# A gated-delta layer: another order within a wave, masks and reductions moved, and layer norms with narrow reciprocals

## The chip, the cores and the metric

The kernel runs on one core of a Trainium2 chip. It is one program of some 48,000 instructions: a model of four layers, all in fp32. The metric is the device time in microseconds. An execution of the kernel before took 2885.48 us (median of three runs, 2884.47 to 2887.69).

## The reference

The input is x of 2 x 512 tokens with 256 channels. Each layer is `x = x + attention(norm(x)) + ffn(norm(x))`. Three layers and all feed-forward parts stay as they are; the change touches the norm, which stands ahead of each layer, and the attention of the last layer, a gated delta rule with 16 key heads, 32 value heads and head width 128:

```python
def _layernorm(x, axis=-1, eps=1e-05):
    m = jnp.mean(x, axis=axis, keepdims=True)
    v = jnp.var(x, axis=axis, keepdims=True)
    return (x - m) / jnp.sqrt(v + eps)
...
            L = -jnp.matmul(kbc, jnp.swapaxes(kc, -1, -2), precision=prec) * decay
            L = jnp.where(tri_incl, 0.0, L)
            attn = solve_triangular(eye - L, jnp.broadcast_to(eye, L.shape), lower=True)
...
                a_i = jnp.matmul(q_i, jnp.swapaxes(k_i, -1, -2), precision=prec) * dm_i
                v_new = v_i - jnp.matmul(kcd_i, state, precision=prec)
                out_i = jnp.matmul(q_i * jnp.exp(g_i)[..., None], state, precision=prec) + jnp.matmul(a_i, v_new, precision=prec)
                new_state = state * jnp.exp(g_last)[..., None, None] + jnp.matmul(jnp.swapaxes(k_i * jnp.exp(g_last[..., None] - g_i)[..., None], -1, -2), v_new, precision=prec)
...
        xf = core.astype(jnp.float32) * jax.nn.silu(z.astype(jnp.float32))
        var = jnp.mean(xf * xf, axis=-1, keepdims=True)
        xf = xf * jax.lax.rsqrt(var + EPS) * norm_weight
        return out @ W_out
```

Queries, keys and values go through a convolution of four taps and a silu first.

## The kernel before, in words

The kernel runs its stages one after the other (`build`). Each norm (`layer_norm`) multiplies with a constant matrix, which puts the mean, and then the variance, of each token on all 128 partitions; ScalarE takes the root of 512 columns at once (L113), VectorE the reciprocal (L94) and the product (L99).

The delta layer (`delta_attention`) works in 64 waves: 16 key heads, and for each four chunks of 128 tokens (CH = 4). A wave holds PR = 4 matrices of 128 x 128: two batches by two value heads. Its steps reach over four turns of the main loop, so in the turn w each engine works for waves w+2, w, w-1 and w-2:

- wave w+2 is made: gates (L1458) and scores (L1468, L1470) on TensorE, `low` (L1871) on VectorE, `decay` and `grown` (L1689, L1692) on ScalarE, then on VectorE `at` and `rough` (L1879), products of the scores with the decay, and `v0` (L1888), the triangular matrix to be inverted, from `rough` and a strict mask. Values and keys are transposed (L1477, L1483) and copied.
- SyncE spreads `v0` through DRAM (L1348, L1354, L1362), so that GpSimd can invert the 16 x 16 diagonal blocks by substitution on 32 partitions (L1823 to L1835, 28 dependent steps and a copy), and gathers the blocks (L1371, L1377).
- for wave w VectorE widens the gathered blocks (L1901) and TensorE joins them to 32, 64 and 128 columns: join_a (L1494), close_a, join_b, close_b, join_c, close_c (L1548), each with copies by ScalarE and VectorE between. The last copy (L1722) gives the inverse.
- for wave w-1 come recall (L1557), rest (L1926), solve (L1565), new values (L1727), the answer (L1575, L1576) and the state's growth (L1582, L1946), the gated output `xf` (L1936), its squares (L1734), their sum (L1953, L1955) and the root to the power -0.5 on GpSimd (L1813).
- for wave w-2 VectorE scales `xf` (`normed`, L1959), TensorE transposes and projects it (L1591, L1602), and VectorE adds it to x (L1967).

Beside this the projections of the next head (L1418, L1428) run as up to four parts a wave, in the PSUM banks BG and BK that the gates and scores of the wave have left. A wave has three parts where w % 4 is 2 or 3, two where it is 0 and four where it is 1; from the last heads on there are none. In the same way VectorE does the four taps of one convolution a wave (L1854, L1857); where w % 4 is 2 its parts come late in the turn.

The order of each engine is written out by hand, as calls in the loop over w. Every engine takes its instructions in this order, and a wait holds all behind it. TensorE's order before is:

```python
make(w + 2); recall(w - 1); join_a(w); part(w, 0)
solve(w - 1); turn_values(w + 2); close_a(w); part(w, 1)
answer(w - 1); join_b(w); part(w, 2); turn_keys(w + 2)
close_b(w); turn_out(w - 2); part(w, 3)
join_c(w); project_out(w - 2); close_c(w)
```

## Time and profile before

| | |
|---|---|
| median of three runs | 2885.48 us (2884.47 to 2887.69) |
| the profiled execution's own time | 2888.33 us |
| its span | 2886.6 us |
| mean granted TensorE clock over the span | 0.907 |
| TensorE busy | 2389.7 us, 83% |
| VectorE busy | 1545.3 us, 54% |
| ScalarE busy | 931.0 us, 32% |
| GpSimd busy | 985.5 us, 34% |

The profiled execution is 2.85 us above the median. Its 1.7 us outside the span stand for what lies around the program. Busy time is an average over all stages, and a busy TensorE can be one at half clock, so the table alone says little of the delta layer; the stretch from 1299.7 to 2811 us is that layer's main loop.

### The profile page before, as it was taken

Reading aid. Unit: us, or ns where it says so; the run is one execution under the profiler, and the core shown is the slowest. Engines: PE = TensorE matmul, PEld = TensorE weight load, DVE = VectorE, ACT = ScalarE, POOL = GpSimd, SP = SyncE. Lnnn points to the kernel's source line nnn. Section 1 sums busy time; section 2 is a strip of 40 time slices with the busy share of each in tenths; the row PEclk is TensorE's granted clock in tenths of the full one; section 3 lists DMA queues with packets and bytes.
Section 4 is the critical chain, followed back from the end, with each engine's and each line's share of the span. In section 5 each row is a group of like instructions: output and inputs, shape, how many; then the busy total and the mean of one; then the engine's idle time right before and its main releaser. Section 6 shows DMA issues by size and latency. Waiting matters only on the chain. (4 is left out here: it accounts for less than half of the span.)

```text
span 2886.6 us, 48059 instructions
## 1 busy us (share of the span) xinstructions
PE 2389.7 (83%) x18052; PEld 1459.9 (51%) x18052; DVE 1545.3 (54%) x2863; ACT 931.0 (32%) x1896; POOL 985.5 (34%) x2123
## 2 busy tenths in 40 slices
PE   6597999986897958747888888888888888888879
PEld 3234444433332425334566656666666666666753
DVE  1632555657753142335666666666666666666531
ACT  1162111101152122123444434444444434443421
POOL 1310001110002001305555555555555555555520
PEclk8798999998798989967999999999999999999989
DMA  1002010101001000011111111111111111111100
GB/s 48 1 0 76 22 37 28 44 0 35 1 1 45 0 28 17 16 31 34 23 36 34 35 27 27 35 37 27 28 35 36 27 34 27 35 38 21 26 13 15
DMA packets 183490, 78.06 MB, mean 27 GB/s; under 512 B 133200, under 2 KB 164464, under 8 KB 183152
## 3 DMA queue, kind: packets, MB, share of 16 engines
q1 hardware_dynamic: 183280, 75.23, 10.0%
q8 instruction: 136, 2.23, 0.3%
q14 instruction: 74, 0.61, 0.1%
HBM read 52.10 MB, written 22.02 MB: 26 GB/s over the span
## 5 line engine op out<-in xcount | busy, mean ns | idle before, releaser
L1832 POOL TENSOR_TENSOR a_z<-a_z,a_term 32x14 f32<-32x14 f32 (+6 forms) x896 | 342.8, 383 | 70.2
L1828 POOL TENSOR_TENSOR a_term<-a_z,a_l 32x14 f32<-32x14 f32 (+6 forms) x896 | 333.6, 372 | 70.2
L1418 PE MATMUL ps<-all_xn,a_w_qkv 128*128 128x512 f32 x512 | 311.4, 743 | 6.2 <-ACT a_grown L1692 4.1
L1005 POOL TENSOR_TENSOR all_x<-all_x,f_part_out 128x512 f32<-128x512 f32 x64 | 85.0, 1365 | 634.3 <-DVE f_part_out L977 634.3
L878 PE MATMUL ps<-all_xn,f_w 128*128 128x512 f32 x640 | 287.8, 594 | 1.9 <-ACT f_share L896 1.9
L1857 DVE SCALAR_TENSOR_TENSOR a_qkv<-a_raw,a_taps,a_qkv 128x1024 f32<-128x1024 f32 x192 | 245.2, 1277 | 2.5
L1823 POOL TENSOR_TENSOR a_z<-a_l,a_ident 32x256 f32<-32x256 f32 x64 | 47.0, 735 | 563.7 <-DMA a_l<-a_v_dram 563.7
L878 PEld LDWEIGHTS ps<-all_xn,f_w 128*128 128x128 f32 x640 | 122.2, 191 | 155.8 <-issue 155.8
L1666 ACT ACTIVATE a_raw<-ps 128x512 f32<-128x512 f32 x128 | 76.5, 597 | 365.8 <-PE ps L1418 365.8
L1494 PE MATMUL ps<-a_t_wide,a_v_off 32*32 32x32 f32 x2048 | 33.9, 211 | 179.9 <-DVE a_t_wide L1901 179.9
L864 PE MATMUL ps<-f_gated,f_w 128*128 128x512 f32 x320 | 155.1, 612 | 20.9 <-DVE f_part_out L977 20.9
L985 DVE TENSOR_TENSOR f_gated<-f_act_h,ps 128x512 f32<-128x512 f32 x80 | 55.0, 688 | 215.0 <-ACT f_act_h L901 214.8
L901 ACT ACTIVATE f_act_h<-ps 128x512 f32<-128x512 f32 x80 | 47.8, 597 | 375.8 <-PE ps L878 375.8
L1428 PE MATMUL ps<-a_w_z,all_xn 128*128 128x256 f32 x512 | 153.3, 453 | 16.8 <-ACT a_zs L1670 16.8
L1602 PE MATMUL ps<-a_out_t,a_w_out 128*128 128x256 f32 x512 | 133.4, 405 | 40.3 <-ACT a_out_t L1740 26.3
L1418 PEld LDWEIGHTS ps<-all_xn,a_w_qkv 128*128 128x128 f32 x512 | 104.1, 223 | 97.2 <-issue 92.0
L1936 DVE SCALAR_TENSOR_TENSOR a_xf<-ps,a_zs 128x512 f32<-128x512 f32 x64 | 44.2, 691 | 190.2 <-PE ps L1576 190.2
L1915 DVE COPY a_za<-ps 32x128 f32<-32x128 f32 x128 | 37.1, 290 | 182.8 <-PE ps L1510 181.9
L1494 PEld LDWEIGHTS ps<-a_t_wide,a_v_off 32*32 32x32 f32 x2048 | 26.1, 122 | 205.6 <-DVE a_t_wide L1901 205.6
L1428 PEld LDWEIGHTS ps<-a_w_z,all_xn 128*128 128x128 f32 x512 | 110.3, 226 | 36.0 <-ACT a_zs L1670 17.2
L1602 PEld LDWEIGHTS ps<-a_out_t,a_w_out 128*128 128x128 f32 x512 | 95.7, 197 | 59.2 <-ACT a_out_t L1740 31.1
L864 PEld LDWEIGHTS ps<-f_gated,f_w 128*128 128x128 f32 x320 | 61.6, 195 | 102.9 <-issue 72.8
(261 smaller groups left out, 4903.3 us busy)
## 6 DMA issues: line engine op xcount, KB each, us to landing
a_v_dram<-a_v SPq DMA_DIRECT2D x64, 256.0 KB, 2.0
f_w<-in_f_w SPq DMA_DIRECT2D x24, 512.0 KB, 4.9
a_w_qkv<-in_a_w SPq DMA_DIRECT2D x16, 512.0 KB, 3.8
a_t_dram<-a_z SPq DMA_DIRECT2D x512, 8.0 KB
a_w_z<-in_a_w SPq DMA_DIRECT2D x16, 256.0 KB, 2.8
a_w_out<-in_a_wo SPq DMA_DIRECT2D x16, 256.0 KB, 2.8
a_v_off<-a_v SPq DMA_DIRECT2D x256, 4.0 KB, 1.8
a_l<-a_v_dram SPq DMA_DIRECT2D x256, 8.0 KB
```

The costliest lines, as they stand in the source:

```text
L864: mm = pe.matmul(ps[:, 4 + b * KC + m, :], w2[:, v, f, m * P:(m + 1) * P], gated[:, (v * TILES + i) % 4, :], start=f == 0, stop=f == FT - 1)
L878: mm = pe.matmul(ps[:, bank + n % 2, :], w[:, v, k, f * P:(f + 1) * P], xn[:, k, b * T:(b + 1) * T], start=k == 0, stop=k == KC - 1)
L985: dve.tensor_tensor(gated[:, n % 4, :], act_h[:, n % 2, :], ps[:, 2 + n % 2, :], ALU.mult).then_inc(gated_ready, 1)
L1005: pool.tensor_tensor(part, part, part_out[:, n, :], ALU.add).then_inc(added, 1)
L1418: mm = pe.matmul(ps[:, to, :], w_qkv[:, k, mt * P:(mt + 1) * P], xn[:, k, b * T:(b + 1) * T], start=k == 0, stop=k == KC - 1)
L1428: mm = pe.matmul(ps[:, to, i * 256:(i + 1) * 256], xn[:, k, tt * P:(tt + 1) * P], w_z[:, k, :], start=k == 0, stop=k == KC - 1)
L1494: mm = pe.matmul(narrow(BW)[q, r, :], v0_off[q, w % 3, r, :], t_wide[q, 1, r, :], start=True, stop=True)
L1602: mm = pe.matmul(bank(BO)[:, B * m:B * (m + 1), :], w_out[:, v, m * P:(m + 1) * P], out_t[:, v::VPK, :], start=v == 0, stop=v == VPK - 1)
L1666: act.activation(raw[:, mt, b, TAPS - 1:], ps[:, of, :], ACT.Copy).then_inc(raw_ready, 1)
L1828: pool.tensor_tensor(term[:, 0:j, j + 1:], z[:, 0:j, j:j + 1].broadcast_to([HP, j, n]), rows[:, j:j + 1, j + 1:].broadcast_to([HP, j, n]), ...
L1832: pool.tensor_tensor(z[:, 0:j, j + 1:], z[:, 0:j, j + 1:], term[:, 0:j, j + 1:], ALU.add).then_inc(sub_step, 1)
L1857: dve.scalar_tensor_tensor(to, rows, tap, to, ALU.mult, ALU.add).then_inc(conv_ready if j == TAPS - 1 else conv_step, 1)
```

## The change

In the loop over w the order of all engines changes. TensorE's `make` is cut in two (`make_gates`, `make_scores`), `answer` in three (`ask`, `answer`, `grow_state`). `rough` and its product go: `v0` is made from the scores in PSUM, the factor and `decay`. This leaves ones' places on its diagonal filled, and GpSimd sets the diagonal to 1.0 after copying the blocks. `at` is made after `v0`. The sums of squares come from an accumulator of ScalarE's Square, one instruction for each of the four matrices. `normed` moves from VectorE to GpSimd, behind `root`. In the norm, variance, root and reciprocal work on one column per 128 tokens, and a product with the identity spreads the result over the partitions in PSUM.

The new orders, as loop bodies (each call stands under its own condition; `late` is w % 4 == 2):

```python
# TensorE
make_gates(w + 2); recall(w - 1); make_scores(w + 2); ask(w - 1)
turn_values(w + 2); solve(w - 1); part(w, 0); join_a(w)
grow_state(w - 1); close_a(w); answer(w - 1); join_b(w)
part(w, 1); close_b(w); turn_out(w - 2); part(w, 2)
turn_keys(w + 2); join_c(w); project_out(w - 2); part(w, 3); close_c(w)
# ScalarE
make_decay(w + 2); grow(w + 2); new_values(w - 1); part(w, 0); copy_tb(w)
make_values(w + 2); silu 0; copy_wb(w); part(w, 1); copy_half(w)
copy_out(w - 2); square(w - 1); silu 1; copy_wc(w); silu 2; part(w, 2)
silu 3; copy_whole(w); part(w, 3); make_keys(w + 2)
# VectorE
make_low(w + 2); make_right(w - 1); make_v0(w + 2); widen(w); make_at(w + 2)
close_wa(w); make_qg(w + 2); copy_za(w); carry(w - 1); gated(w - 1)
conv 0 (late: conv 0, 1, 2); copy_z_half(w); conv 1, 2, 3 (late: none)
reduce(w - 1); late: conv 3; add_out(w - 2)
# GpSimd
substitute(w + 2); root(w - 1); normed(w - 1)
```

The core of the diff:

```diff
@@ layer_norm, TensorE, VectorE, ScalarE @@
-                    for k in range(KC):
-                        mm = pe.matmul(ps[:, B + b, :], mean_of[:, :], square[:, k, b * T:(b + 1) * T],
-                                       start=k == 0, stop=k == KC - 1)
+                    for tt in range(b * ST, (b + 1) * ST):
+                        for k in range(KC):
+                            mm = pe.matmul(ps[:, B + b, tt:tt + 1], square[:, k, tt * P:(tt + 1) * P],
+                                           mean_of[:, 0:1], start=k == 0, stop=k == KC - 1)
+                for b in range(B):
+                    pe.wait_ge(rstd_ready, b + 1)
+                    for q in range(ST):
+                        tt = b * ST + q
+                        mm = pe.matmul(ps[:, 2 * B + b, q * P:(q + 1) * P],
+                                       rstd[:, tt:tt + 1].to_broadcast([P, P]), ident[:, :], start=True, stop=True)
+                    mm.then_inc(spread, 1)
-                    dve.reciprocal(std[:, b, :], std[:, b, :]).then_inc(rstd_ready, 1)
+                    dve.reciprocal(rstd[:, of], rstd[:, of]).then_inc(rstd_ready, 1)
-                        dve.tensor_tensor(xn[:, k, part], xn[:, k, part], std[:, b, :],
+                        dve.tensor_tensor(xn[:, k, part], xn[:, k, part], ps[:, 2 * B + b, :],
-                    act.activation(std[:, b, :], ps[:, B + b, :], ACT.Sqrt,
+                    act.activation(rstd[:, of], ps[:, B + b, of], ACT.Sqrt,
@@ delta_attention, TensorE @@
                 def turn_values(w):
                     if w >= 1:
                         pe.wait_ge(krow_ready, PR * w)
+                    if w % CH == 0:
+                        pe.wait_ge(qkv_ready, 4 * (w // CH) + 3)
-                def answer(w):
-                    pe.wait_ge(vnew_ready, PR * (w + 1))
-                    pe.wait_ge(at_ready, w + 1)
+                def ask(w):
+                    pe.wait_ge(state_ready, PR * (w + 1))
                     pe.wait_ge(qg_ready, w + 1)
                     if w >= 2:
                         pe.wait_ge(added, w - 1)
                     for r in range(PR):
-                        pe.matmul(bank(BO)[:, r, :], qg[:, w % 4, r, :], state[:, r, :], start=True, stop=False)
+                        mm = pe.matmul(bank(BO)[:, r, :], qg[:, w % 4, r, :], state[:, r, :],
+                                       start=r == 0, stop=False)
+                    mm.then_inc(asked, 1)
+
+                def answer(w):
+                    pe.wait_ge(vnew_ready, PR * (w + 1))
+                    pe.wait_ge(at_ready, w + 1)
+                    for r in range(PR):
                         mm = pe.matmul(bank(BO)[:, r, :], at[:, w % 4, r, :], v_new[:, r, :],
-                                       start=False, stop=True)
+                                       start=False, stop=r == PR - 1)
                     mm.then_inc(o_psum, 1)
+
+                def grow_state(w):
                     if w % CH == CH - 1:
                         return
+                    pe.wait_ge(vnew_ready, PR * (w + 1))
@@ project_out @@
                     pe.wait_ge(ot_ready, w + 1)
+                    if w >= 1:
+                        pe.wait_ge(added, w)
@@ ScalarE, square @@
-                    act.activation(sq[:, :, :], xf[:, :, :], ACT.Square).then_inc(sq_ready, 1)
+                    for r in range(PR):
+                        act.activation(sq[:, r, :], xf[:, r, :], ACT.Square,
+                                       accum_out=sums[:, r:r + 1]).then_inc(sq_ready, 1)
@@ GpSimd @@
+                def normed(w):
+                    pool.wait_ge(rstd_ready, w + 1)
+                    if w >= 1:
+                        pool.wait_ge(ot_psum, w)
+                    pool.tensor_tensor(xnorm[:, :, :], xf[:, :, :],
+                                       rstd[:, :].unsqueeze(2).broadcast_to([P, PR, P]), ALU.mult
+                                       ).then_inc(xnorm_ready, 1)
-                    pool.tensor_tensor(z16[:, w % 2, 0, :], l16[:, w % 2, :], ident16[:, :],
-                                       ALU.add).then_inc(sub_step, 1)
+                    pool.tensor_copy(z16[:, w % 2, 0, :], l16[:, w % 2, :]).then_inc(sub_step, 1)
+                    pool.wait_ge(sub_step, steps * w + 1)
+                    pool.memset(z16[:, w % 2, 0, ::SB + 1], 1.0).then_inc(sub_step, 1)
@@ VectorE @@
                 def make_v0(w):
-                    dve.wait_ge(rough_ready, w + 1)
+                    dve.wait_ge(kq_ready, w + 1)
+                    dve.wait_ge(decay_ready, w + 1)
                     for r in range(PR):
-                        dve.scalar_tensor_tensor(v0[:, w % 3, r, :], rough[:, r, :], gate(K_NBETA, w, r),
-                                                 strict[:, :], ALU.mult, ALU.mult).then_inc(v0_ready, 1)
+                        dve.scalar_tensor_tensor(v0[:, w % 3, r, :], bank(BK)[:, r // VPK, :], gate(K_NBETA, w, r),
+                                                 decay[:, r, :], ALU.mult, ALU.mult).then_inc(v0_ready, 1)
@@ carry @@
                     if w % CH == CH - 1:
+                        dve.wait_ge(asked, w + 1)
                         dve.memset(state[:, :, :], 0.0).then_inc(state_ready, PR)
@@ reduce @@
-                    dve.tensor_reduce(var[:, :], sq[:, :, :], AX.X, ALU.add).then_inc(var_step, 1)
-                    dve.wait_ge(var_step, w + 1)
-                    dve.tensor_scalar(var[:, :], var[:, :], 1.0 / P, 1e-6, ALU.mult, ALU.add).then_inc(var_ready, 1)
+                    dve.tensor_scalar(var[:, :], sums[:, :], 1.0 / P, 1e-6, ALU.mult, ALU.add).then_inc(var_ready, 1)
@@ build @@
+                sp.dma_start(ident[:, :], d["ident"]).then_inc(arrived, 16)
```

## Rows read from the trace of the kernel before

**Rows 1.** Windows: busy us and instructions of each engine, clock, DMA share, GB/s.
```profile
1351.10:2683.50 1332.40, 1137.28 (x13005) 862.56 (x13003) 851.71 (x1838) 576.79 (x1286) 755.28 (x1787) 0.92 0.14 31
```
**Rows 2.** Timeline of TensorE: start us, us, the gates' product, first of a wave.
```profile
1351.12 1.24 PE L1458 MATMUL ps<-a_upto,a_gates 128*128 128x128 f32 x8
...
2683.48 1.16 PE L1458 MATMUL ps<-a_upto,a_gates 128*128 128x128 f32 x8
```
**Rows 3.** Waits, 1320 to 2720 us: total us, times, longest.
```profile
PE ps L1494 <- DVE a_t_wide L1901: 171.2, 60, 8.9
```
**Rows 4.** Timeline of TensorE over one wave with four projections.
```profile
2013.80 0.45 PE L1494 MATMUL ps<-a_t_wide,a_v_off 32*32 32x32 f32 x32 [2.75 <-DVE a_t_wide L1901]
2014.18 3.68 PE L1428 MATMUL ps<-a_w_z,all_xn 128*128 128x256 f32 x8
...
2024.75 1.99 PE L1428 MATMUL ps<-a_w_z,all_xn 128*128 128x256 f32 x8
2026.58 0.38 PE L1483 MATMUL ps<-a_ident,a_qkv 128*128 128x128 f32 x2
...
2032.71 1.16 PE L1458 MATMUL ps<-a_upto,a_gates 128*128 128x128 f32 x8
2033.71 0.61 PE L1468 MATMUL ps<-a_qkv 128*128 128x128 f32 x4
...
2038.38 0.65 PE L1494 MATMUL ps<-a_t_wide,a_v_off 32*32 32x32 f32 x32 [2.74 <-DVE a_t_wide L1901]
```
**Rows 5.** Timelines of ScalarE (first line) and VectorE (the others), one wave.
```profile
2049.38 0.62 ACT L1734 ACTIVATE a_sq<-a_xf 128x512 f32<-128x512 f32 x1
...
2057.59 1.12 DVE L1871 SCALAR_TENSOR_TENSOR a_low<-ps,a_gates,a_floor 128x128 f32<-128x128 f32 x4
2059.25 1.12 DVE L1926 SCALAR_TENSOR_TENSOR a_rest<-ps,a_gates,a_v_row 128x128 f32<-128x128 f32 x4 [0.53 <-PE ps L1557]
...
2060.89 0.68 DVE L1879 TENSOR_TENSOR a_rough<-ps,a_decay 128x512 f32<-128x512 f32 x1
2061.48 0.41 DVE L1901 TENSOR_TENSOR a_t_wide<-a_t_narrow,a_side 128x256 f32<-128x256 f32 x1
```
**Rows 6.** Timelines of SyncE, GpSimd and VectorE; last line: durations min/median/max of L1005.
```profile
2039.40 0.34 SPq L1348 DMA_DIRECT2D a_v_dram<-a_v  x1
...
2044.98 5.99 SPq L1371 DMA_DIRECT2D a_t_dram<-a_z  x8
2046.32 0.72 POOL L1823 TENSOR_TENSOR a_z<-a_l,a_ident 32x256 f32<-32x256 f32 x1 [8.43 <-DMA a_l<-a_v_dram]
...
2049.61 0.27 POOL L1828 TENSOR_TENSOR a_term<-a_z,a_l 32x50 f32<-32x50 f32 x1
...
2052.35 0.36 SPq L1377 DMA_DIRECT2D a_t_narrow<-a_t_dram  x1
...
2056.40 1.28 DVE L1857 SCALAR_TENSOR_TENSOR a_qkv<-a_raw,a_taps,a_qkv 128x1024 f32<-128x1024 f32 x1
2056.54 1.30 POOL L1832 TENSOR_TENSOR a_z<-a_z,a_term 32x50 f32<-32x50 f32 x1
...
2061.01 1.01 POOL L1813 TENSOR_TENSOR a_rstd<-a_var,a_half 128x4 f32<-128x4 f32 x1
...
L1005 POOL TENSOR_TENSOR all_x<-all_x,f_part_out x64: 1261/1271/2297, 346.8 to 1208.2; 128x512 f32<-128x512 f32 x64
```
**Rows 7.** Timeline of TensorE: two waves without projections.
```profile
2701.92 1.16 PE L1458 MATMUL ps<-a_upto,a_gates 128*128 128x128 f32 x8
...
2720.23 1.16 PE L1458 MATMUL ps<-a_upto,a_gates 128*128 128x128 f32 x8
```
**Rows 8.** Timeline of the last norm.
```profile
1218.86 1.28 ACT L113 ACT_TABLE_LOAD   x1
...
1218.90 1.98 PE L79 MATMUL ps<-n_square,all_mean_of 128*128 128x512 f32 x4 [0.25 <-ACT n_square L108]
...
1220.88 3.35 DVE L94 RECIPROCAL n_std<-n_std 128x512 f32<-128x512 f32 x1 [2.70 <-ACT n_std L113]
...
1228.86 1.29 DVE L99 TENSOR_TENSOR all_xn<-all_xn,n_std 128x512 f32<-128x512 f32 x2
```

More of the change, by code:

```diff
@@ L92, in _ @@
                 for b in range(B):
+                    of = slice(b * ST, (b + 1) * ST)
                     dve.wait_ge(std_ready, b + 1)
-                    dve.reciprocal(std[:, b, :], std[:, b, :]).then_inc(rstd_ready, 1)
-                    dve.wait_ge(rstd_ready, b + 1)
+                    dve.reciprocal(rstd[:, of], rstd[:, of]).then_inc(rstd_ready, 1)
+                for b in range(B):
+                    dve.wait_ge(spread, b + 1)
                     dve.wait_ge(squared, KC * (b + 1))
@@ L1249, in delta_attention @@
         zs = s.buf("zs", [P, 2, TT, VPK * P])
-        low, decay, grown, rough = (s.buf(n, [P, PR, P]) for n in ("low", "decay", "grown", "rough"))
+        low, decay, grown = (s.buf(n, [P, PR, P]) for n in ("low", "decay", "grown"))
         v0, v0_off = s.buf("v0", [P, 3, PR, P]), s.buf("v0_off", [P, 3, PR, HP])
@@ L1460, in make, with make_scores @@
                     mm.then_inc(gc_ready, 1)
+                def make_scores(w):
+                    before = parts_of(w - 3)
                     if before:
@@ L1463, in make @@
                     elif w >= 1:
-                        pe.wait_ge(rough_ready, w)
+                        pe.wait_ge(v0_ready, PR * w)
+                        pe.wait_ge(at_ready, w)
                     if w % CH == 0:
@@ L1626, in _ @@
                     if made(w + 2):
-                        make(w + 2)
+                        make_gates(w + 2)
                     if made(w - 1):
                         recall(w - 1)
+                    if made(w + 2):
+                        make_scores(w + 2)
+                    if made(w - 1):
+                        ask(w - 1)
+                    if made(w + 2):
+                        turn_values(w + 2)
+                    if made(w - 1):
+                        solve(w - 1)
+                    part(w, 0)
                     if made(w):
                         join_a(w)
-                    part(w, 0)
                     if made(w - 1):
-                        solve(w - 1)
-                    if made(w + 2):
-                        turn_values(w + 2)
+                        grow_state(w - 1)
                     if made(w):
                         close_a(w)
-                    part(w, 1)
                     if made(w - 1):
@@ L1643, in _ @@
                         join_b(w)
+                    part(w, 1)
+                    if made(w):
+                        close_b(w)
+                    if made(w - 2):
+                        turn_out(w - 2)
                     part(w, 2)
@@ L1647, in _ @@
                     if made(w):
-                        close_b(w)
-                    if made(w - 2):
-                        turn_out(w - 2)
-                    part(w, 3)
-                    if made(w):
                         join_c(w)
@@ L1655, in _ @@
                         project_out(w - 2)
+                    part(w, 3)
                     if made(w):
@@ L1801, in _ @@
                         copy_whole(w)
+                    part(w, 3)
+                    if made(w + 2):
+                        make_keys(w + 2)
             @block.gpsimd
@@ L1830, in substitute @@
                                            ALU.mult).then_inc(sub_step, 1)
-                        pool.wait_ge(sub_step, steps * w + 2 * j)
+                        pool.wait_ge(sub_step, steps * w + 2 * j + 1)
                         pool.tensor_tensor(z[:, 0:j, j + 1:], z[:, 0:j, j + 1:], term[:, 0:j, j + 1:],
@@ L1842, in _ @@
                         root(w - 1)
+                        normed(w - 1)
             @block.vector
@@ L2010, in _ @@
                 for w in range(-2, W + 2):
+                    late = w % CH == 2
                     if made(w + 2):
@@ L2019, in _ @@
                     if made(w + 2):
-                        make_v0(w + 2)
-                    if made(w - 2):
-                        normed(w - 2)
+                        make_at(w + 2)
                     if made(w):
                         close_wa(w)
-                    late = w % CH == 2
-                    if not late:
-                        conv(w, 0)
+                    if made(w + 2):
+                        make_qg(w + 2)
                     if made(w):
```

129 lines of the change are left out of this document (65 added, 64 removed).

## Prediction

> **What bounds the kernel now.** The windows view comes first. It shows the delta layer's steady part, from 1351.1 to 2683.5, as 1332.4 us in which TensorE is busy 1137, GpSimd 755, VectorE 852 and ScalarE 577, at a mean granted clock of 0.92 [rows 1]: TensorE is nearest to full, and it is the one whose stalls I look for. The marks that bound this part are the same instruction, the first of a wave, 57 waves apart [rows 2]: 1332.4 / 57 = 23.4 us a wave. In the waits of this stretch TensorE has one long one, at the join of the inverse (L1494) for the widened blocks (L1901): 171.2 us in 60 times, 2.85 each [rows 3].
>
> TensorE's timeline shows the rest of that stall [rows 4]. The wave from 2013.80 to 2038.38 (24.58 us, four projections) holds the idle gap of 2.74, and the projection right behind the gap takes 3.68 where the same work takes 1.99 later in the wave. Double the time is the lower of the two clock levels, 1.2 in place of 2.4 GHz: behind each gap TensorE works at half clock, and 1.69 more is lost. What is left, 24.58 - 2.74 - 1.69 = 20.15, is the wave's work at full clock. Two of the four kinds of wave have one projection less (1.83, from 2024.75 to 2026.58), so 18.3; one has two less and no state growth (as many passes as the gates' product, 1.0 from 2032.71 on), so 15.5. The mean of the four is **18.07 us**: TensorE's floor, 5.3 below today's wave.
>
> Why TensorE waits: VectorE makes low, rest, at and rough and only then widens, 2057.59 to 2061.48, 3.89 us with 0.5 of waiting for the recall in it [rows 5]. TensorE has only scores and recall to do beside that.
>
> **The change, part by part.**
>
> *The order within a wave.* I lay the steps on a line from the end of close_c, with these durations. TensorE: gates to 1.0, recall 1.9, scores 2.8, ask 3.7, values turned 4.2. VectorE: low 1.1 to 2.2, rest to 3.3, v0 to 4.4 (ScalarE's decay, of the size of the 0.62 square, lies beside rest), widen to 4.8. The solve wants rest (3.3) and finds it; then comes the first projection, 5.1 to 6.9, which wants grown (3.5); the join then wants the widened blocks (4.8). **The stall is gone, with 2 us to spare**: widening moved up on VectorE, and the join moved behind ask, values, solve and a projection. In one wave of four ScalarE reloads a table ahead of the exponential, 1.28 [rows 8], which moves v0 and widen to 5.7, still ahead of the join. Without the gap there is no half clock. Further down each copy now has a product of another chain in front of the product that wants it: projection 1 between join_b and close_b, projection 2 or the keys between turn_out and project_out. I followed all waits: new_values ends at 6.4, growth wants it at 7.3; the gated output is done near 11.5, project_out wants it at 16; VectorE's add_out ends near 0.5 of the next wave, the ask wants it at 2.8. So the new waits (ask and project_out on the add, carry on the ask, turn_values on the keys, which ScalarE now copies last) find their semaphore up. Queued behind them, if not: behind the ask the solve, and with it everything; behind carry VectorE's gated output. What is late next is rest, 0.9 ahead of the solve. In every fourth wave, the one with late convolutions, copy_z_half stands behind three of them, near 16.8, and close_c wants it at 17.7.
>
> Gain: 57 x (23.4 - 18.07) = 302 us at the floor. For hand-overs that my line has too smooth I charge 0.4 a wave, 23 us: **279**.
>
> *VectorE's load.* rough (0.68) goes; v0 reads PSUM and decay in place of rough and mask, in four instructions like low's (1.12): the same. The reduction and the normed output go as well, tiles of rough's size. 852 / 57 = 14.9 a wave less 3 x 0.68 is 12.9, under 15.5 even with gaps: this is cover, not a term. It is worth 0 while TensorE bounds; if it were missing, the short wave would wait for VectorE by 1 to 2 us.
>
> *Sums of squares on ScalarE.* One instruction of 0.62 [rows 5] becomes four with an accumulator, a form the trace lacks. Bounds: 0 more, and 4 x 0.62 - 0.62 = 1.9. I take 0.6, since each works on a quarter and only its start is paid four times. ScalarE is busy 577 of 1332, so it hides: 0.
>
> *GpSimd.* It gets the normed output; the same tile in a two-input operation costs 1.27 at the median and 2.3 at most [rows 6]; I take 1.3, these being the same size. The identity addition becomes a copy and a small memset: even. Its wave was 2046.32 to 2061.01, 14.7, and 1.0 for the root; it becomes 14.7 + 1.0 + 1.3 + small gaps = **17.1**, 95% of TensorE's 18.07. It starts 6.9 behind the first DMA of its wave (2039.40 to 2046.32). So normed ends 6.9 + 17.1 = 24 behind v0, near 10.5 of the next wave, where gated (10.7) just finds it; in short waves gated waits 1 to 2 us, which VectorE's slack takes. SyncE issues the same DMAs in the same order; none is moved past another. Price 0, with rival A below.
>
> On the port the trace shows contention: a 50-element GpSimd operation takes 1.30 beside VectorE's convolution step and 0.27 alone [rows 6]. The Trainium skill ("SBUF — State Buffer", section "SBUF: two separate sides") calls the shared port pair an exclusive lock, held for the whole instruction, so that the other side fully blocks. It speaks against moving work to GpSimd: by that rule a convolution that meets the normed output waits for it, up to 1.3 on VectorE a wave, and with VectorE at 12.9 + 1.3 the sum stays as it is.
>
> *Waves without projections.* The last ones took 18.3 (2701.92 to 2720.23) [rows 7], mostly latency. On the same line they come to 14.3, and GpSimd, without three stretched steps, to 14.7 - 3 + 1.0 + 1.3 = 14. Four of them, and a little in the four that drain: **17** (10 to 25). The first two waves wait for the first inverse as before: 0.
>
> *The four norms.* The last part is a reciprocal over 512 columns, 3.35 us, twice, and four products, 1220.88 to 1230.15 [rows 8]. Now root and reciprocal take four columns, TensorE turns the result into rows (eight passes a half, like the gates' product, 1.0), and the products read PSUM. The line: table loaded 1220.1, variances of the second half to 1220.8, spread to 1221.8 and 1222.8, products to 1224.4: 5.7 saved. At half clock the narrow products double, and 3.6 is saved. x4: **22** (14 to 23). The identity's load at the start rides beside the 1 MB of x: 0 to 1.
>
> *Sum*, against the profiled execution's own 2888.3: 2888.3 - 279 - 17 - 22 = 2570. That execution is 2.8 above the median of the runs; taken off, the forecast is **2568 us**. The rivals below are on the same footing.
>
> **The rivals.**
>
> *A. GpSimd becomes the bound.* For it: 17.1 against 18.07, and steps stretched by 1 us; the normed output could meet convolutions and take 2.3. Then GpSimd's wave is 18.1, and with what the chain gated, convolutions, low, v0 adds some 19.5: 57 x 3.9 = 222, sum 2624. Against: VectorE drops two operations that used the port.
>
> *B. A stall of some 2 us comes back elsewhere*, at the solve (for rest) or the ask (for the add), with half clock behind it: 21 a wave, 57 x 2.4 = 137, sum 2709. For it: VectorE's chain add, low, rest has under 1 us to spare. Against: the line above.
>
> *C. The order brings nothing*, because the wave is really held by the round of v0: 6.9 to GpSimd, 14.7 of steps, then the stores and the load (2044.98 to 2052.35, 7.4, and 2 to land [rows 6]), 31 us over two waves, 15.5 a wave. That is below 18, so it can hardly hold; only the norms would gain, 2863.
>
> *D. Slower.* One place: the normed output on GpSimd, behind the dependent steps and the root. It decides where GpSimd's wave passes 24.1, today's wave plus what tail and norms give back: 24.1 - 15.8, so 8.3 us for that operation. The root of only four elements costs 1.01 [rows 6], so GpSimd's prices can surprise; at 10 us the wave is 25.8, 2885.5 + 57 x 2.4 - 39 = 2983. Against it stands the 1.27 of a tile of the same size.
>
> **Chances.** Forecast 0.58; A 0.23; B 0.13; C 0.03; D 0.02; 0.01 for the rest. The forecast's own range is 2537 (no charge for hand-overs, 25 in the tail) to 2600. Taking in A with its spread gives 2537 to 2660, with B, C and D outside. Slower is D, 0.02; within 0.2% (5.8 us, about what a measurement of this kernel can tell from no change) 0.01; faster 0.97.
>
> **What the profile of the changed kernel would show.** TensorE's wait for widen gone; the gates' first marks 18 to 19 apart on average, 15.5 to 20 by kind of wave; granted clock near 1.0 in the steady part; all projections at 1.83; GpSimd busy over 85% of it, its DMA wait under 2 us a wave; VectorE's gated output waiting for the normed one in some waves; normed at 1.3; each norm near 13.5 from first product to last. The forecast is wrong if TensorE shows a new idle of 2 us a wave before solve, ask or project_out, or if GpSimd has no wait for its DMA left.

## The result, and the profile after

| | before | after |
|---|---|---|
| median | 2886.56 us (4 runs, 2884.47 to 2887.69) | 2551.61 us (4 runs, 2546.98 to 2560.84) |
| ratio, 95% interval | | 0.8844 [0.8818, 0.8871] |
| profiled execution: time, span | 2888.33, 2886.6 | 2553.82, 2552.0 |
| granted clock over the span | 0.907 | 0.939 |

335 us are gone; 318 were forecast (2885.5 to 2568), and 2551.6 lies inside the range. The kernel after was timed again later (after_again): 2552.16 us (5 runs), ratio 0.8837 [0.8825, 0.8850]. To read the numbers below one thing is needed: 13 of the 58 executions of kernels with the new norm, and none of the 57 with the old one, took 20 to 27 us more than their kernel's others, in the two that were profiled ahead of the last norm, for a cause that no run here isolates (it may be a price of the new norm), so where a kernel's spread is wide I read its delta layer from the profile.

The windows view after, with the columns of [rows 1]. The first stretch is the filling of the delta layer, the second its 57 steady waves, the third the rest of its loop, the waves without projections and the draining ones:

```profile
1285.60:1333.90 48.30, 33.01 (x242) 19.24 (x242) 23.71 (x46) 14.14 (x30) 26.62 (x73) 0.79 0.12 25
1333.90:2372.50 1038.60, 1032.51 (x13004) 805.08 (x13002) 753.88 (x1669) 616.84 (x1684) 804.58 (x1884) 1.00 0.18 41
2372.50:2476.50 104.00, 87.27 (x1286) 74.33 (x1284) 48.95 (x142) 47.02 (x157) 56.98 (x157) 0.95 0.11 23
```

The 57 waves of [rows 1] took 1332.4 us and now take 1038.6, 18.22 each in place of 23.4. TensorE is busy 1032.5 us of them at a granted clock of 1.00, the upper level; before it was busy 1137.3 at 0.92. So both parts of the old stall went: 195.1 us of idle time (1332.4 - 1137.3) are down to 6.1, and 104.8 us of busy time (1137.3 - 1032.5) are gone too, for as many instructions, so it is what the half clock had added. The 335 us split, by the two profiles, into waves 293.8, everything ahead of the loop 14.1 (it starts at 1285.61 in place of 1299.72), filling 3.1 and tail 23.6.

TensorE's timeline of a short wave, a gates' product to the next, to be held against [rows 4]:

```profile
1972.61 1.16 PE L1473 MATMUL ps<-a_upto,a_gates 128*128 128x128 f32 x8
...
1976.69 1.06 PE L1586 MATMUL ps<-a_rest,a_inv 128*128 128x128 f32 x8
1977.59 1.88 PE L1432 MATMUL ps<-all_xn,a_w_qkv 128*128 128x512 f32 x4
1979.40 0.45 PE L1515 MATMUL ps<-a_t_wide,a_v_off 32*32 32x32 f32 x32
1980.28 0.45 PE L1527 MATMUL ps<-a_t_wide,a_wa 32*32 32x32 f32 x32 [0.42 <-DVE a_wa L1964]
...
1988.65 1.16 PE L1473 MATMUL ps<-a_upto,a_gates 128*128 128x128 f32 x8
```

The join (L1515) stands 6.8 us behind the wave's start and waits for nothing. The only idle time is 0.42 at close_a (L1527), for the copy of the join's own result: this wave has no growth between the two. The four waves from 1954.29 on take 18.32, 16.04, 20.08 and 18.32; by kind I had read 18.3, 15.5, 20.15 and 18.3 out of [rows 4].

VectorE's timeline (first line: widen in the wave that starts at 1954.29; second line: the copy behind join_a), and the waits of the steady part:

```profile
1958.60 0.41 DVE L1956 TENSOR_TENSOR a_t_wide<-a_t_narrow,a_side 128x256 f32<-128x256 f32 x1
...
1961.61 0.29 DVE L1964 TENSOR_TENSOR a_wa<-ps,a_ident 128x128 f32<-128x128 f32 x1 [2.00 <-PE ps L1515]
```

```profile
DVE a_wa L1964 <- PE ps L1515: 97.6, 57, 2.4
POOL a_z L1875 <- DMA a_l<-a_v_dram: 96.9, 37, 5.5
...
DVE a_xf L1991 <- POOL a_xnorm L1863: 21.5, 21, 1.7
```

Widen ends 4.7 us behind the wave's start (4.8 on my line), 2 us ahead of the join. The direction of the wait of [rows 3] has turned: it is VectorE that now waits for the join, 1.7 us a wave, while TensorE idles 6.1 us in the 57 waves together. GpSimd still waits for its DMA, 96.9 / 57 = 1.7 us a wave, so it is no bound. VectorE waits for the normed output 21 times, 21.5 us in all.

GpSimd's timeline shows what was given to it:

```profile
1961.65 1.01 POOL L1857 TENSOR_TENSOR a_rstd<-a_var,a_half 128x4 f32<-128x4 f32 x1
1962.74 1.04 POOL L1863 TENSOR_TENSOR a_xnorm<-a_xf,a_rstd 128x512 f32<-128x512 f32 x1
1966.42 0.39 POOL L1875 COPY a_z<-a_l 32x256 f32<-32x256 f32 x1 [2.63 <-DMA a_l<-a_v_dram]
...
1982.91 0.39 POOL L1875 COPY a_z<-a_l 32x256 f32<-32x256 f32 x1
```

The wave from the first copy to the second is 16.5 us long (17.1 forecast), and GpSimd waits for nothing in it.

The last norm, against [rows 8]:

```profile
1199.37 6.39 PE L76 MATMUL ps<-all_x,all_mean_of 128*128 128x512 f32 x8 [7.17 <-PEq L41]
...
1205.60 1.84 PE L83 MATMUL ps<-all_mean_of,n_square 128*128 128x1 f32 x16
...
1207.80 3.17 PE L83 MATMUL ps<-all_mean_of,n_square 128*128 128x1 f32 x16 [0.36 <-ACT n_square L121]
...
1210.83 3.76 PE L90 MATMUL ps<-all_ident,n_rstd 128*128 128x128 f32 x16
1211.01 0.26 ACT L127 ACTIVATE n_rstd<-ps,n_eps 128x4 f32<-128x4 f32 x1 [1.68 <-PE ps L83]
1211.30 0.18 DVE L106 RECIPROCAL n_rstd<-n_rstd 128x4 f32<-128x4 f32 x1 [1.77 <-ACT n_rstd L127]
1212.92 1.28 DVE L112 TENSOR_TENSOR all_xn<-all_xn,ps 128x512 f32<-128x512 f32 x2 [1.44 <-PE ps L90]
1214.63 1.28 DVE L112 TENSOR_TENSOR all_xn<-all_xn,ps 128x512 f32<-128x512 f32 x2 [0.42 <-PE ps L90]
```

The windows view over the second half's variances and over the spread (the clock is the third number from the end):

```profile
1208.00:1211.00 3.00, 3.00 (x17) 3.00 (x17) 0.18 (x1) 1.31 (x2) 0.00 (x0) 0.54 0.02 5
1211.00:1215.00 4.00, 3.59 (x16) 3.30 (x16) 1.83 (x4) 0.26 (x1) 0.00 (x0) 0.50 0.00 0
```

The reciprocal of 3.35 us is down to 0.18. But sixteen one-column passes of the variance take 3.17 us the second time and 1.84 the first, and the spread (L90), sixteen passes of a kind of which eight take 1.0 in a wave, takes 3.76. The granted clock is 1.00 from 1205.6 to 1208, then 0.54 and 0.50: the spread stands at half clock, and so does nearly all of the second half's variance. This norm takes 16.5 us from its first product to the end of its last multiplication, 19.3 before. It is the one of the four that gained least: the others take 14.0, 13.7 and 12.4 us in place of 19.2, 19.2 and 17.4.

### The profile page after: what moved, and what is told of

Same layout as the page of the kernel before. It is cut to its first block and busy times, and to the rows that moved or that the text cites. A ratio compares the mean times of both kernels' runs of the same rounds, so it can differ in the third digit from the quotient of the medians.

```text
span 2552.0 us, 49069 instructions
## 1 busy us (share of the span) xinstructions
PE 2292.4 (90%) x18212; PEld 1420.6 (56%) x18212; DVE 1403.0 (55%) x2671; ACT 973.6 (38%) x2344; POOL 1046.1 (41%) x2251
## 5 line engine op out<-in xcount | busy, mean ns | idle before, releaser
L1432 PE MATMUL ps<-all_xn,a_w_qkv 128*128 128x512 f32 x512 | 251.0, 617 | 5.3 <-ACT a_grown L1733 4.0
L1442 PE MATMUL ps<-a_w_z,all_xn 128*128 128x256 f32 x512 | 125.9, 390 | 16.8 <-ACT a_zs L1708 16.8
L1432 PEld LDWEIGHTS ps<-all_xn,a_w_qkv 128*128 128x128 f32 x512 | 90.6, 195 | 78.5 <-issue 76.7
L1442 PEld LDWEIGHTS ps<-a_w_z,all_xn 128*128 128x128 f32 x512 | 96.0, 195 | 29.7 <-ACT a_zs L1708 17.2
L1768 ACT ACTIVATE a_v_new<-ps,a_gates 128x128 f32<-128x128 f32 x256 | 73.2, 368 | 91.7 <-PE ps L1586 91.6
L1925 DVE SCALAR_TENSOR_TENSOR a_low<-ps,a_gates,a_floor 128x128 f32<-128x128 f32 x256 | 72.0, 344 | 63.3 <-PE ps L1473 63.3
L1875 POOL COPY a_z<-a_l 32x256 f32<-32x256 f32 x64 | 26.5, 414 | 189.8 <-DMA a_l<-a_v_dram 189.6
L587 POOL TENSOR_TENSOR a_heads<-a_mixed,a_recip 128x512 f32<-128x512 f32 x8 | 10.1, 1268 | 226.6 <-DVE a_recip L653 226.6
L280 ACT ACTIVATE a_probs<-ps 128x512 f32<-128x512 f32 x128 | 65.8, 606 | 78.6 <-PE ps L245 78.6
```

What stands on the lines that cost most here:

```text
L1432: mm = pe.matmul(ps[:, to, :], w_qkv[:, k, mt * P:(mt + 1) * P], xn[:, k, b * T:(b + 1) * T], start=k == 0, stop=k == KC - 1)
L1442: mm = pe.matmul(ps[:, to, i * 256:(i + 1) * 256], xn[:, k, tt * P:(tt + 1) * P], w_z[:, k, :], start=k == 0, stop=k == KC - 1)
L1768: act.activation(v_new[:, r, :], bank(BR)[:, r, :], ACT.Copy, scale=gate(K_BETA, w, r)).then_inc(vnew_ready, 1)
L1925: dve.scalar_tensor_tensor(low[:, r, :], bank(BG)[:, r, :], gate(K_GC, w, r), floor[:, :], ALU.subtract, ALU.min).then_inc(low_ready, 1)
```

## The experiments

Each is named by its label. Line numbers shift by a few between kernels. The ratio is against the kernel before, 0.8844 being the change's own. "Steady part" is the stretch of the 57 waves, 1038.6 us in the change. Each diff shows the core of its edit.

**norms_only.** The kernel before with the new norm and nothing else.

```diff
 # before, layer_norm as in the change
+        ident = s.buf("ident", [P, P])
+                sp.dma_start(ident[:, :], d["ident"]).then_inc(arrived, 16)
-                sp.wait_ge(arrived, 32)
+                sp.wait_ge(arrived, 48)
```

> The kernel before with the new layer norm and nothing else. Theory (the profile after): each norm gives back 3.3 us and not 5.7, since the narrow products run at half clock; four of them give 13, so 2873 us against 2886.5. Rival (the term as it was summed): 22, so 2864. A third: the gain of the norms is inside the delta layer too, by the clock that it starts with: over 25.

Measured: 2872.76 us (12 runs), ratio 0.9971 [0.9946, 0.9997], 14 less than the 2886.81 measured beside it. That agrees with the first theory's 13, but not with its "3.3 us each": in this kernel's profile the norms take 16.5, 13.4, 12.3 and 16.5 us, 2.6, 5.7, 5.1 and 2.7 less than before. So the gain is not the same at each place.

**full_var.** The change, with 128 equal columns moving in the variance products where it has one. ScalarE reads one in 128 of them.

```diff
-                            mm = pe.matmul(ps[:, B + b, tt:tt + 1], square[:, k, tt * P:(tt + 1) * P],
-                                           mean_of[:, 0:1], start=k == 0, stop=k == KC - 1)
+                            q = tt - b * ST
+                            mm = pe.matmul(ps[:, B + b, q * P:(q + 1) * P], square[:, k, tt * P:(tt + 1) * P],
+                                           mean_of[:, :], start=k == 0, stop=k == KC - 1)
-                    act.activation(rstd[:, of], ps[:, B + b, of], ACT.Sqrt,
+                    act.activation(rstd[:, of], ps[:, B + b, ::P], ACT.Sqrt,
```

> The kernel after with one thing changed in the norm: the variance's products take 128 equal columns of the mean matrix as the moving side instead of one, at the same number of passes, and ScalarE reads one column of each. Theory (the narrow products leave TensorE's array so little to do that the clock falls behind them): the passes stay at 0.11 us, the clock stays up, the spread takes 1.9 and not 3.8 us, and 2 to 3 us are saved in each norm, 8 to 12 in all, 2542. Rival (the clock falls for another reason, so wide passes at half clock cost what they did): 0 to 4 us more. The difference is near what a comparison can tell, so the norm's own rows decide.

The timeline of its last norm (L84 the variances, L91 the spread):

```profile
1205.90 2.05 PE L84 MATMUL ps<-all_mean_of,n_square 128*128 128x128 f32 x16 [0.26 <-ACT n_square L122]
...
1207.79 1.95 PE L91 MATMUL ps<-all_ident,n_rstd 128*128 128x128 f32 x16
...
1208.89 2.48 DVE L113 TENSOR_TENSOR all_xn<-all_xn,ps 128x512 f32<-128x512 f32 x4 [0.42 <-PE ps L91]
```

Products 128 times as wide take less time: 2.05 in place of 3.17, and the spread behind them 1.95 in place of 3.76. The granted clock is 1.00 from 1205.90 to 1211.00, where the change had 0.54 and 0.50. So it was the narrow products, by the clock behind them, that had cost the last norm its missing time: it takes 13.8 us here and 16.5 in the change. The whole kernel: 2547.54 us (5 runs), ratio 0.8827 [0.8815, 0.8839], 4.6 under the change timed beside it; the two intervals overlap, so the rows are the proof and not the median. The forecast of 8 to 12 was too high, for it took every norm to lose what the last one does: the four take 13.6, 13.8, 11.6 and 13.8 us, 3.9 less in all, 2.7 of it in the last. It is the fastest version of this study.

**widen_early.** The kernel before with one call moved: widening ahead of the scores' copies on VectorE.

```diff
+                    if made(w):
+                        widen(w)
                     if made(w + 2):
                         make_scores(w + 2)
-                    if made(w):
-                        widen(w)
```

> The kernel before with one call moved: VectorE widens ahead of at and rough, so the join's wait should fall from 2.85 us to some 1.5. Theory (clock follows the gap's length): a gap of 1.5 us leaves TensorE at full clock, so 1.3 + 1.7 = 3.0 us a wave, 57 waves, some 170 us and about 2715 us in all. Rival (any gap in front of the join halves the clock behind it): only 1.3 a wave, 75 us, 2810. Rival of no gain: at and rough, later by 0.4, hold the next projection: under 20 us.

Measured: 2793.91 us (4 runs, 2784.19 to 2799.68), ratio 0.9684 [0.9668, 0.9701], 93 less; the profiled execution is the fastest of the four. Its timeline of TensorE, its waits and the window of its 57 steady waves:

```profile
1897.74 0.45 PE L1494 MATMUL ps<-a_t_wide,a_v_off 32*32 32x32 f32 x32 [1.55 <-DVE a_t_wide L1901]
1898.13 1.98 PE L1418 MATMUL ps<-all_xn,a_w_qkv 128*128 128x512 f32 x4
```

```profile
PE ps L1494 <- DVE a_t_wide L1901: 89.5, 57, 2.0
...
DVE a_xnorm L1959 <- POOL a_rstd L1813: 38.2, 32, 3.7
...
PE ps L1506 <- DVE a_wa L1909: 35.1, 32, 3.5
```

```profile
1351.99:2577.90 1225.91, 1063.00 (x13005) 820.81 (x13003) 863.60 (x1838) 581.27 (x1286) 752.76 (x1780) 0.98 0.15 34
```

The gap shrank from 2.75 to 1.55, and the projection behind it takes 1.98, not 3.68: behind the shorter gap TensorE kept the upper clock. By both together 3 us a wave should have gone, 170 in all. In this profile's steady part 106 went (1332.4 - 1225.9), 1.9 a wave: 74 as busy time (1137.3 - 1063.0) and 32 as idle time, for the join's wait fell by 67 (156.9 in the same stretch before), and 35 came back as a new wait, close_a for wa (L1506). It comes from VectorE, which waits 38.2 us for GpSimd's root ahead of that very wa (L1959), 4.7 before. The median lies near the rival's 2810, but the rows are against that rival, since the clock behind the join stayed up. One call moved gives about a third of the gain; the rest is in the other moves.

**join_early.** The change with the join moved up behind the ask, ahead of the values, the solve and the projection.

```diff
-                    if made(w):
-                        join_a(w)
                     if made(w - 1):
                         grow_state(w - 1)
...
                         ask(w - 1)
+                    if made(w):
+                        join_a(w)
                     if made(w + 2):
                         turn_values(w + 2)
```

> The kernel after with one call moved back: join_a behind ask, ahead of the transposed values, the solve and the first projection. The widened blocks are ready 4.7 us into a wave and the ask ends at 3.6, so TensorE idles 1.1 (2 where the table is reloaded), 1.35 on average. Theory (short gaps keep the clock): 57 x 1.35 = 77 us more than the kernel after, 2630. Rival (half clock comes back with any gap): 1.7 more a wave, 2725. Rival (the join's place is not what removed the stall): no change, 2552.

Measured: 2653.99 us (4 runs), ratio 0.9185 [0.9169, 0.9202], 102 more than the change. Timelines of three waves, wait and window of the steady part:

```profile
1896.11 0.45 PE L1515 MATMUL ps<-a_t_wide,a_v_off 32*32 32x32 f32 x32 [0.96 <-DVE a_t_wide L1956]
...
2013.41 0.65 PE L1515 MATMUL ps<-a_t_wide,a_v_off 32*32 32x32 f32 x32 [2.76 <-DVE a_t_wide L1956]
...
2014.90 1.91 PE L1586 MATMUL ps<-a_rest,a_inv 128*128 128x128 f32 x8
...
2171.59 0.45 PE L1515 MATMUL ps<-a_t_wide,a_v_off 32*32 32x32 f32 x32 [2.76 <-DVE a_t_wide L1956]
...
2172.47 1.06 PE L1586 MATMUL ps<-a_rest,a_inv 128*128 128x128 f32 x8
```

```profile
PE ps L1515 <- DVE a_t_wide L1956: 80.4, 57, 2.8
```

```profile
1354.69:2481.24 1126.55, 1046.11 (x13004) 818.80 (x13002) 754.27 (x1669) 616.70 (x1684) 798.28 (x1886) 0.99 0.16 37
```

The stall is back in all waves, at 80.4 / 57 = 1.4 us, as forecast. The steady part is 88 us longer: 74 of idle time and 14 of busy time (1046.1 against 1032.5), since some of the longer gaps, not all, were followed by half clock. Of two gaps of 2.76 us one has the solve behind it at 1.91 us and the other at 1.06. So the time lost is in the main the waiting itself; half clock behind every gap, at the 1.7 a wave of the kernel before, would have added 97 more. The tail gives the other 13. This one place in the order is worth 102 us, where the forecast had 77, for it had left out the half clock and the tail.

**order_alone.** The new order with the old work: old norm, `rough` and mask, one Square and a reduction, and the normed output on VectorE, behind close_wa. Only GpSimd's diagonal stays as in the change, a copy and a small memset.

```diff
 # the change, with the old norm and the pieces of one_square, rough_back and normed_dve
```

> The new order and waits, with all operations as before: rough and the strict mask, one square and VectorE's reduction, the normed output on VectorE, the old norms. Theory (the order is the whole of the delta layer's gain, the rest is cover): 2552 + 13 for the norms, and up to 15 where VectorE, at some 15 us a wave, is late in the waves of 16: 2565 to 2580. Rival (the lighter VectorE is needed for it): widening is 0.7 later and each convolution too, 1 us a wave and more, 2625 or above.

Measured: 2604.28 us (5 runs), ratio 0.9022 [0.901, 0.9035], 52 above the change, between the theory and its rival. Its VectorE timeline shows why:

```profile
1879.14 0.69 DVE L1996 TENSOR_TENSOR a_xnorm<-a_xf,a_rstd 128x512 f32<-128x512 f32 x1 [1.63 <-POOL a_rstd L1843]
```

The wait for GpSimd's root holds all that VectorE has behind it: 87.8 us, 46 times.

**normed_dve.** The change with only the normed output back on VectorE, at the same place.

```diff
 # VectorE's loop; `normed` itself as on GpSimd, with dve for pool
                         close_wa(w)
+                    if made(w - 2):
+                        normed(w - 2)
```

> The kernel after with the normed output back on VectorE, behind close_wa. Theory (it is cover: VectorE has 5 us of slack a wave): within 10 us of the kernel after. GpSimd's wait for its DMA rises by 1.1 a wave and VectorE's wait for the normed output before gated goes. Rival (the move is part of what bought the gain, since VectorE's short wave is full): 0.5 to 1 us a wave, 30 to 57 us more.

Measured: 2579.25 us (6 runs, 2562.33 to 2595.59), ratio 0.8946 [0.8916, 0.8976]; the same wait, 57.6 us, 32 times. The spread is wide, and the profiled execution, 2562.33, has a steady part of 1047.7 us: 9.1 more than the change, within the theory's 10 and not the median's 27.

**normed_dve_late, order_alone_late.** The same two kernels with `normed` put between carry and gated, about 3 us further down.

```diff
-                    if made(w - 2):
-                        normed(w - 2)
...
                         carry(w - 1)
+                    if made(w - 2):
+                        normed(w - 2)
+                    if made(w - 1):
                         gated(w - 1)
```

> The kernel after with the normed output back on VectorE as in normed_dve, but just ahead of gated, two steps later in VectorE's wave (behind qg, za and carry). In normed_dve VectorE waited 51.5 us for GpSimd's root in the window, with za and carry queued behind it. Theory (it was the place of the wait that cost, not the 0.68 us of work): within 5 us of the kernel after, 2550 to 2558. Rival (the work itself does, VectorE is full in the short waves): as normed_dve, 2562 or more.

> As order_alone, with the normed output just ahead of gated. Theory (of the 38 us between order_alone and the kernel after that are not the norms', the wait for the root ahead of za is most): 2575 to 2585. Rival (it is VectorE's 2.0 us more work a wave): 2600, as before.

Measured: normed_dve_late 2557.57 us (6 runs), ratio 0.887 [0.8842, 0.8898], its steady part 1038.6 us, as in the change. order_alone_late 2572.04 us (5 runs), ratio 0.8917 [0.89, 0.8934]. Its window and its wait for the root:

```profile
1345.60:2389.64 1044.04, 1035.09 (x13004) 804.12 (x13003) 874.85 (x1839) 580.17 (x1285) 748.61 (x1824) 1.00 0.17 40
```

```profile
DVE a_xnorm L1996 <- POOL a_rstd L1843: 3.7, 7, 0.6
```

The wait fell from 87.8 to 3.7 us, and 32 us went with it (21 of them in the steady part, 1064.8 to 1044.0). What had cost time was the place of the wait and not VectorE's work. And **the order alone, with the operations as before but for GpSimd's copy and memset, is worth 2885.6 - 2572.0 = 313.5 us** of 333.4, the distance to the change's 2552.16 of after_again. Of the 20 left the norms take 14; the normed output on GpSimd, the accumulators and the dropped `rough` share 6. In the steady part they are worth 5.4 (1044.0 against 1038.6), although VectorE is 121 us less busy (874.9 against 753.9).

**one_square.** The change with one Square and VectorE's reduction.

```diff
-                    for r in range(PR):
-                        act.activation(sq[:, r, :], xf[:, r, :], ACT.Square,
-                                       accum_out=sums[:, r:r + 1]).then_inc(sq_ready, 1)
+                    act.activation(sq[:, :, :], xf[:, :, :], ACT.Square).then_inc(sq_ready, 1)
...
+                    dve.tensor_reduce(sums[:, :], sq[:, :, :], AX.X, ALU.add).then_inc(var_step, 1)
+                    dve.wait_ge(var_step, w + 1)
```

> The kernel after with one Square over the whole tile on ScalarE and the sum by VectorE's reduction. Theory (cover on both): VectorE gets 0.7 us more a wave ahead of add_out, low and rest, which has under 1 us to spare, so 0 to 10 us more. Rival (the reduction on VectorE is late for the solve in the short waves): 0.5 us in every wave, 30 more. Rival on the other side (four squares and four reads of the accumulator, 1.5 us on ScalarE, held copy_wc): 5 to 10 us less.

Measured: 2560.58 us (6 runs), ratio 0.8887 [0.8859, 0.8916]; steady part 1041.9, 3.3 more than the change. That is the theory's 0 to 10.

**rough_back.** The change with `rough` and the strict mask.

```diff
+                    score(w, 0, rough[:, :, :]).then_inc(rough_ready, 1)
+                    dve.wait_ge(rough_ready, w + 1)
-                        dve.scalar_tensor_tensor(v0[:, w % 3, r, :], bank(BK)[:, r // VPK, :], gate(K_NBETA, w, r),
-                                                 decay[:, r, :], ALU.mult, ALU.mult).then_inc(v0_ready, 1)
+                        dve.scalar_tensor_tensor(v0[:, w % 3, r, :], rough[:, r, :], gate(K_NBETA, w, r),
+                                                 strict[:, :], ALU.mult, ALU.mult).then_inc(v0_ready, 1)
```

> The kernel after with rough and the strict mask as before, so that v0 and the widened blocks are 0.6 to 0.7 us later in a wave. Theory: the join has 2 us to spare for widen, so 0 to 5 us in the steady waves, and 5 to 8 in the waves without projections, where v0 starts the round through DRAM: 2555 to 2563. Rival (v0's place sets the wave through GpSimd, since the normed output is then 0.7 later for gated): 0.5 a wave, 30 more.

Measured: 2572.27 us (6 runs, 2561.09 to 2583.46), ratio 0.8905 [0.8878, 0.8933]. The median says 20; the profile says otherwise. In it the last norm, ahead of everything that this edit touches, starts at 1224.40 in place of 1199.37. Its steady part is 1042.4 us, 3.8 more than the change's, and its tail is no longer. So `rough` in the delta layer costs 4 us, and the median of this kernel can't be used for more than a bound.

**pool_load2.** The change with two more products of the normed output's size on GpSimd in each wave. Their results are not used.

```diff
+                    for e in range(2):
+                        if w or e:
+                            pool.wait_ge(spared, 2 * w + e)
+                        pool.tensor_tensor(spare[:, :, :], xf[:, :, :],
+                                           rstd[:, :].unsqueeze(2).broadcast_to([P, PR, P]), ALU.mult
+                                           ).then_inc(spared, 1)
                     pool.tensor_tensor(xnorm[:, :, :], xf[:, :, :],
```

> The kernel after with two more products of the normed output's shape on GpSimd each wave, into a spare tile, ahead of the normed output. GpSimd's wave goes from 16.5 to some 18.7 us against TensorE's 18.22. Theory (GpSimd stands just under the bound): GpSimd sets the wave, 18.8 to 19.2, 35 to 60 us more, 2590 to 2610, its wait for its DMA gone and TensorE idle again. Rival (there is much slack behind GpSimd): under 10 us more.

Measured: 2605.12 us (4 runs), ratio 0.9045 [0.9015, 0.9075], 53 more. The window of its steady part and the waits for the normed output there:

```profile
1335.59:2414.73 1079.14, 1040.63 (x13004) 808.66 (x13002) 748.44 (x1669) 617.59 (x1684) 923.85 (x1993) 1.00 0.17 39
```

```profile
DVE a_xf L1998 <- POOL a_xnorm L1870: 113.0, 55, 3.7
...
PE ps L1622 <- POOL a_xnorm L1870: 29.5, 26, 1.5
```

2.1 us more work on GpSimd makes a steady wave (1079.1 - 1038.6) / 57 = 0.7 longer and the tail 10 in all: about 1.4 us of slack were left on GpSimd, and then it bounds, through the waits of the gated output and of TensorE's turn_out for the normed one. GpSimd's own wait for its DMA fell from 96.9 us to 13.6. Rival A was 1.4 us of GpSimd's work a wave away.

## Why the prediction was right

**The stall and the half clock: right.** 57 waves were to give 302 at TensorE's floor of 18.07; they gave 293.8 at 18.22. The charge of 0.4 a wave for hand-overs was the wrong size: it measured 0.15, most of it the 0.42 before close_a in the waves without growth (0.1 on the mean of four), which my line had overlooked. join_early puts a shorter stall back, and the time comes with it: 80 us of waiting, 102 in all. widen_early takes part of the old stall away, and shows that the wait's length alone doesn't give the time: new waits took back 35 us.

**The floor as mean of four kinds of wave: right,** but for the short one, 16.0 in place of 15.5.

**VectorE's relief is cover and worth 0: right in size, and narrower than I put it.** 121 us less work brought 5 in the steady part. The half-sentence on short waves that "would wait for VectorE by 1 to 2 us" was too much. What I had not seen is that a *wait* on VectorE can cost more than its work does: the normed output behind close_wa costs 9 us (normed_dve, steady part) to 32 (order_alone against order_alone_late), and about three microseconds further down nothing that could be measured. Moving it to GpSimd removes the question, for there it stands behind the root on the same engine.

**GpSimd: right that it doesn't bound, and off on its numbers.** Its wave is 16.5 in place of 17.1: the copy that replaced the identity's addition takes 0.39 where the addition took 0.72, and the normed output 1.04 where I had taken 1.3 from a tile with two full inputs [rows 6]. It is busy 804.6 of 1038.6 us, 77%, where I had said over 85%: that is 14.1 a wave, and the rest of the 16.5 are short gaps between dependent steps, which are not counted busy. The sign that I named with it held: its wait for the DMA is 1.7 a wave, under 2.

The rule of the Trainium skill that I had weighed ("SBUF — State Buffer", section "SBUF: two separate sides") is an exclusive lock, under which a convolution would wait for the normed output. In this profile it could not show there: none of the 64 normed outputs meets a convolution, and the 192 convolution steps behind the first tap take 1.285 us at the median and 1.464 at most. It shows at another instruction of VectorE, the product `qg` (L1948), which reads two tiles in SBUF, and of which the first two lines are an example, the third one without the meeting:

```profile
1761.81 1.04 POOL L1863 TENSOR_TENSOR a_xnorm<-a_xf,a_rstd 128x512 f32<-128x512 f32 x1
1761.87 1.52 DVE L1948 TENSOR_TENSOR a_qg<-a_qkv,a_grown 128x512 f32<-128x512 f32 x1
...
1889.08 0.68 DVE L1948 TENSOR_TENSOR a_qg<-a_qkv,a_grown 128x512 f32<-128x512 f32 x1
```

Where `qg` begins during a normed output, 14 times in the profile, it takes up to 1.52 us in place of 0.68 and ends 0.55 us behind the normed output's end, whenever it began. The 14 cost VectorE 8 us together. GpSimd loses in its turn: its 26-element steps take 1.29 beside a convolution and 0.22 alone. And a normed output that began 0.04 us behind `qg` took 1.53 in place of 1.04. The trace agrees with the lock, held by whichever began first; VectorE does lose by it here, and its slack covers the loss.

**Squares: right.** Four squares of 0.297 and four readings of the accumulator of 0.189, partly overlapped, span 1.26 us in place of 0.62; I had put 0.6 more. ScalarE hides it.

**The norms: the term that failed in size.** I had 22 (14 to 23), four times the 5.7 that I read on the last norm's line. By the two profiles the norms are 5.1, 5.5, 4.9 and 2.7 us shorter, 18.2 in all; the stages between them took 4 us more, so that the loop starts 14.1 sooner, and norms_only gives 14 by its median. The step at fault stands in the line of the last norm: "variances of the second half to 1220.8, spread to 1221.8 and 1222.8". It prices both at full clock, the spread by eight passes inside a wave. Measured there are 3.17 for the variances in place of 1.9 and 3.76 for the spread in place of 2.0, for the spread follows 32 passes of one column each, and the granted clock falls during them. Even my half-clock bound, 3.6 saved, was too good for this norm. full_var shows the cause by giving the columns back. The other three came near the 13.5 that I had named, and carry most of the term.

**Tail and filling.** The tail gave 23.6, near the upper end of 10 to 25: its waves are 14.4 to 15.4 us apart (marks at 2372.50, 2386.88, 2402.26 and 2417.37), a little above the 14.3 of the forecast, and the draining waves gave more than "a little". The filling gave 3.1 where I had put nothing.

**The sum.** 293.8 + 14.1 + 3.1 + 23.6 = 334.6 against 279 + 22 + 0 + 17 = 318. Three terms were 15, 3 and 7 too low and one 8 too high. The forecast was 16 us (0.6%) too slow, chiefly by the charge for hand-overs; that it came so near is in part luck, since the error on the norms took off half of that charge's.

## What to carry to other kernels

Read the floor of a wave from the bounding engine's own timeline, with the idle gap and the slow instruction behind it taken off; an order that hides the gap came within 1% of that floor here, and the exchanged operations beside it were worth 6 us of 334. When a calculation moves between engines, ask first where its wait stands in the order of the engine that gets it: three microseconds in place were worth 9 to 32 us here, the 0.7 us of work nothing measurable. Narrowing TensorE's products to one column slowed what came behind them. And price a part that occurs four times at each of its four places: the norm that I had read was the one that gained least.

## What the runs showed of the hardware that I had not expected

- A gap of 2.75 us on TensorE was followed by a projection at half clock, 3.68 us in place of 1.98, and one of 1.55 (widen_early) was not. The gap's length doesn't settle it: in join_early the gaps are 0.96 to 2.76 us, and of two of 2.76 one was followed by half clock and the other was not (the solve behind them 1.91 and 1.06 us).
- Behind products with one moving column and a 128-column weight load the granted clock fell from 1.00 to 0.50: sixteen such passes take 1.84 us and the next sixteen 3.17, and the sixteen 128-column passes behind them 3.76. With 128 columns moving the clock stays at 1.00, and the same steps take 2.05 and 1.95.
- A product of two SBUF tiles on VectorE that begins during GpSimd's normed output takes up to 1.52 us in place of 0.68, and ends 0.55 us behind the other's end.
- The output of ScalarE's accumulator is an instruction of its own, 0.189 us behind each square of 0.297.
- GpSimd's product of a 128x512 tile with a broadcast operand takes 1.04 us, the sum of two such full tiles 1.27; its root of four elements takes 1.01, about as much as the product of 512.
